# A Macaron layer on one core: the feed-forwards' output as split products in the two row halves of TensorE, their input in two runs, and another order of the work on every engine

## The chip, the core and the metric

The kernel runs on one core of a Trainium2 chip. A core has TensorE (PE: matrix products into PSUM, a memory of eight banks of 128 x 512 float32), VectorE (DVE), ScalarE (ACT), GpSimd (POOL) and SyncE (SP), which issues the transfers. The engines run side by side, each through its own instructions in order, and wait for each other only at semaphores. The metric is the device time of the one core in microseconds (us). Changes of under about 0.2% cannot be told from no change here.

## The reference

The input x is 16 x 1024 rows of 512 float32 channels. All weights are shared by the rows.

```python
def ffn(x):                                   # used twice, with the same weights
    s = x @ Win + bin_                        # 512 -> 64
    h = relu(s[..., None] * W1 + b1)          # 64 -> 64 x 16
    g = einsum('btmh,mh->btm', h, W2) + b2    # -> 64
    return g @ Wout + bout                    # 64 -> 512

def attn(x):                                  # 16 heads of 32 channels
    q, k, v = split(x @ w_attn)               # 512 -> 3 x 512
    q, k = elu(q) + 1, elu(k) + 1
    # causal linear attention:
    #   S_t = S_(t-1) + k_t v_t^T,  z_t = z_(t-1) + k_t
    #   y_t = (q_t S_t) / (q_t . z_t + 1e-6)
    return y @ w_proj

x = x + 0.5 * ffn(layernorm(x))
x = x + attn(layernorm(x))
x = x + 0.5 * ffn(layernorm(x))
```

## The kernel before

The 16384 rows are cut into 32 blocks of 512 rows, each of four tiles of 128 rows; two blocks are one batch item, so the running state starts anew in every even block. A program without loops on the device is written out for `j` = 0 to 33. In turn `j` the attention works on block `j`, the first feed-forward (called `1` or `L1`) on block `j + 2` and the second (`0` or `L3`) on block `j - 1`. Both feed-forwards of a turn share their instructions: the second lies in partitions 0 to 63, the first in 64 to 127.

Products. Everything with 512 channels (`project` for q and k, `values`, `outer` for the output projection) is done by `split3` (L916) as three products in the type float32r: high part times high part, high times low, low times high. ACT makes the high part with a copy, DVE or POOL the low part with a subtraction. All other products (`ff_in`, `ff_out`, the transposes `key` and `channels`, `den`, `spread`, `scores`, `attend`, `update`) are float32; the profile lists each of these as two matmuls, but for the transposes, of which it lists one. `ff_in` (L934) multiplies 32 x 64 pieces, so that eight of them, in four row groups and two column halves of the array, are in flight. `ff_out` (L944) is one product per tile and half: 64 rows of `ffs` (the sums g) by `wo`, 128 x 512 out.

A turn on PE: q and k of five channel groups, `ff_in`, the other three groups with `key` and `den` (the denominators q . z; `den` 0 and 1 together, 2 and 3 after six more product groups), `values`, `spread` (reciprocals of the denominators, spread to all channels), and then for each tile `scores`, `attend`, `update` and `outer`, with `channels` (transposes for the next block) in between. The eight `ff_out` stand around the last `outer`.

Between them: ACT turns q and k through `Relu` and `Exp` (L448, L450), does the normalisations (L413), the 16 `hidden` activations of the feed-forwards (L432), and the high parts and copies (L390). DVE does the 16 `hidden` sums (L647, L650), half of the masks on the scores (L702), the statistics (L616, L618), the low parts (L632), the running key sums along the rows (`zsum`, L681: a scan of 512 elements into one of the two buffers `z2`, which starts from the carried sum `zc`), the reciprocals (`rec`, L687, L689), q times the reciprocals (`qnorm`, L694) and all additions to the rows (L657, L725). POOL copies the last column of each scan to `zc` (L320), multiplies the scan by q (L322), adds the half bias (`bias`, L314), computes the deviations (L296, L298) and does the other masks (L326).

The order on each engine is written by hand. PSUM banks go to products by `give`: always the bank that was given away longest ago. The scans 2 and 3 reuse the buffers of scans 0 and 1, so they wait for `den` 0 and 1 (`s_den`, L677). `ff_out` waits for the last `hidden` sum (`s_hm`), the attention products wait for all masks of their tile (`s_am`), and the scores of a tile for the low part of the result of the tile before (`s_yl`), since these use the same four banks `att`.

Of the kernel before, what the change touches and what calls it, by code (L numbers as in the profile page):

```python
# [10 lines left out]
P = 128  # L11
TILES = 4
BLK = P * TILES
SLOTS = 5
D = 32
# [25 lines left out]
def macaron_kernel(nc, x, w_attn, w_proj, Win, bin_, W1, b1, W2, b2, Wout, bout, out):  # L41
# [9 lines left out]
    with ctx:  # L51
# [10 lines left out]
        wo = sb("wo", [P, C])  # L62
# [15 lines left out]
        ktok = [sb(f"ktok{i}", [P, C]) for i in range(2)]  # L78
# [16 lines left out]
        att = ctx.enter_context(nc.psum_tensor("att", [P, 4, 512], F32))  # L95
        psum = ctx.enter_context(nc.psum_tensor("acc_psum", [P, BLK], F32))
# [16 lines left out]
        s_fi, s_fs, s_hr, s_hm = (sem(f"s_{n}") for n in ("fi", "fs", "hr", "hm"))  # L113
# [30 lines left out]

        def reads_none(b, t):
            return b % PER == 0 and t == 0

# [7 lines left out]
        def emptied(kind, b, i):  # L155
# [15 lines left out]
            return {"v": s_v, "key": s_ktok, "xT": s_xTl, "y": s_x2, "sc": s_yl}[kind], 4 * b + i + 1  # L171
# [3 lines left out]
        def give(among, *products):  # L175

            for kind, b, i in products:
                there = on(b) and not (kind in ("o0", "o1") and (kind, b, i) in spot) and not (kind == "up" and not updates(b, i))
# [16 lines left out]
        for j in range(NB + 2):  # L195
            give(ATT + RING, ("q", j, 0), ("k", j, 0), ("k", j, 1), ("q", j, 1), ("k", j, 2))
            if on(j - 1) or on(j + 2):
                give_all("in", j, 0)
            give(ATT + RING, ("k", j, 3), ("q", j, 2), ("key", j, 0), ("den", j, 0), ("q", j, 3), ("v", j, 0),
                 ("v", j, 1), ("key", j, 1))  # L200
            for t in range(TILES):
# [3 lines left out]
            give(RING, ("v", j, 3), ("xT", j + 1, 0), ("up", j, 0), ("xT", j + 1, 1), ("key", j, 2))  # L205
            give_all("sc", j, 1)
            give(RING, ("xT", j + 1, 2), ("y", j, 0), ("xT", j + 1, 3), ("up", j, 1))
            give_all("sc", j, 2)
            give(RING, ("y", j, 1), ("up", j, 2), ("key", j, 3))
            give_all("sc", j, 3)  # L210
            give(RING, ("y", j, 2))
            give(ATT + RING, ("up", j, 3), ("o0", j - 1, 0), ("o1", j + 2, 0), ("y", j, 3), ("o0", j - 1, 1),
                 ("o0", j - 1, 2), ("o1", j + 2, 1), ("o1", j + 2, 2), ("o0", j - 1, 3), ("o1", j + 2, 3))
# [10 lines left out]
        def _(eng):  # L224
# [11 lines left out]
            for h in range(2):  # L236
                eng.dma_start(wo[M * h:M * h + M, :], Wout).then_inc(s_wo, 16)
# [30 lines left out]
        def _(eng):  # L268
# [39 lines left out]

            def bias(half, b, t):
# [6 lines left out]
            def zsum(b, g):  # L316
# [3 lines left out]
                eng.tensor_copy(zc[:, g:g + 1], z[:, BLK - 1:BLK]).then_inc(s_zc, 1)  # L320
# [11 lines left out]
            for b in range(2):  # L332
                for t in range(TILES):
                    bias(1, b, t)
# [8 lines left out]
            for j in range(NB + 2):  # L343
# [5 lines left out]
                if on(j):  # L349
                    zsum(j, 0)  # L350
# [822 lines left out]
```

## Time and profile before

| | us |
|---|---|
| median of 3 runs (lowest, highest) | 2559.25 (2556.72, 2559.64) |
| the profiled execution, its own time | 2556.46 |
| its span, first to last instruction | 2554.7 |
| PE busy | 2373.4 (93%) |
| DVE busy | 1892.7 (74%) |
| ACT busy | 1422.0 (56%) |
| POOL busy | 867.4 (34%) |

A matmul's listed duration is its latency; the next one starts before it ends. What a matmul costs its engine is the distance from its start to the next start. The mean granted clock of TensorE over the span is 0.983.

### The profile page before, as it was taken

The numbers are of one execution on the slowest core, as the hardware profiler recorded it, in microseconds if no ns is written. First come the engines' busy times: TensorE is split into PE (matmuls) and PEld (weight loads), VectorE is DVE, ScalarE is ACT, GpSimd is POOL, SyncE is SP. The second block draws the span as 40 slices with busy tenths as digits, with TensorE's granted clock in tenths as the row PEclk, the third lists the DMA queues.
The fourth block names the chain that finished last, engine by engine and source line by source line (L and its number), as shares of the span: only waits on it lengthen the run. The fifth ranks groups of instructions, "written<-read, shape, count | busy, mean of one in ns | idle before, by whom it ended". The sixth has DMA issues, their size and how long they took to land.

```text
span 2554.7 us, 75807 instructions
## 1 busy us (share of the span) xinstructions
PE 2373.4 (93%) x33282; PEld 1799.6 (70%) x33282; DVE 1892.7 (74%) x3248; ACT 1422.0 (56%) x2248; POOL 867.4 (34%) x996
## 2 busy tenths in 40 slices
PE   2799999999999999999999999999999999999995
PEld 1577777777777777777777777777777777777773
DVE  4578777778777778777777877777877777877755
ACT  3456565556565555556555656555656555556544
POOL 4332333333333333233333233333333333323221
PEclk8899999999999999999999999999999999999997
DMA  5000011001011111001110001111100111000000
GB/s 161 1 2 25 12 35 35 35 35 35 2 35 35 35 35 35 18 19 35 35 35 35 35 2 35 35 35 35 35 3 34 35 35 35 35 18 2 18 18 34
DMA packets 39355, 76.97 MB, mean 30 GB/s; under 512 B 4081, under 2 KB 4081, under 8 KB 39026
## 3 DMA queue, kind: packets, MB, share of 16 engines
q1 hardware_dynamic: 39026, 72.12, 8.2%
q8 instruction: 263, 4.31, 0.7%
q14 instruction: 66, 0.54, 0.1%
HBM read 38.56 MB, written 33.55 MB: 28 GB/s over the span
## 4 chain that ended last, share of the span: by engine, by line
PE 86%; DVE 5%; ACT 4%; issue 3%; SPq 0%; POOL 0%; DMA 0%; DVEq 0%; POOLq 0%
PE bank L916 31%; PE att L916 27%; PE att L934 6%; PE att L1010 6%; PE att L1035 4%; PE att L944 3%; DVE yl L632 3%; ACT yh L390 2%; PE att L1026 2%; PE bank L951 2%; PE att L981 1%; PE att L968 1%; PE bank L944 1%; DVE acc_psum L650 1%; ACT v L390 1%
## 5 line engine op out<-in xcount | busy, mean ns | idle before, releaser
L413 ACT ACTIVATE xhat<-res,nmr,rstd 128x512 f32<-128x512 f32 x384 | 303.0, 806 | 324.2 <-DVE nmr L623 297.0
L432 ACT ACTIVATE ffr<-ffs,b1c,w1c 128x512 f32<-128x512 f32 (+1 forms) x544 | 430.6, 810 | 17.5 <-DVE acc_psum L650 7.9
L650 DVE SCALAR_TENSOR_TENSOR acc_psum<-ffr,w2c,acc_psum 128x512 f32<-128x512 f32 (+1 forms) x476 | 354.4, 745 | 49.4 <-ACT ffr L432 34.2
L326 POOL TENSOR_SCALAR_AFFINE_SELECT A<-A 128x512 f32<-128x512 f32 x256 | 158.7, 637 | 683.7 <-ACT A L390 683.7
L314 POOL TENSOR_TENSOR res<-res,hbout 128x512 f32<-128x512 f32 x256 | 325.1, 1288 | 127.6 <-ACT xhat L413 127.6
L616 DVE BATCH_NORM_STATS2 st<-res 128x6 f32<-128x512 f32 x384 | 261.7, 682 | 17.1 <-DMA res<-in_L_attn_x_dram 8.8
L916 PE MATMUL att<-xh,wa_h 128*128 128x512 f32 x560 | 228.8, 408 | 15.4 <-DVE xl L632 15.4
L390 ACT ACTIVATE A<-att 128x512 f32<-128x512 f32 x256 | 142.5, 596 | 145.8 <-PE att L1010 143.4
L916 PE MATMUL att<-xl,wa_h 128*128 128x512 f32 x560 | 221.9, 396 | 0.0
L916 PE MATMUL att<-xh,wa_l 128*128 128x512 f32 x560 | 221.8, 396 | 0.0
L702 DVE TENSOR_TENSOR A<-att,tri 128x512 f32<-128x512 f32 x256 | 171.9, 683 | 57.2 <-PE att L1010 57.1
L934 PE MATMUL att<-xf,win 32*64 32x128 f32 x8192 | 149.8, 281 | 61.5 <-issue 41.0
L670 DVE SCALAR_TENSOR_TENSOR kT<-bank,kT 128x512 f32<-128x512 f32 x67 | 46.4, 692 | 208.8 <-ACT kT L450 208.7
L296 POOL TENSOR_SCALAR nmr<-mv 128x4 f32<-128x4 f32 x96 | 22.1, 230 | 520.2 <-DVE mv L618 520.1
L934 PEld LDWEIGHTS att<-xf,win 32*64 32x64 f32 x8192 | 135.1, 136 | 83.2 <-issue 75.4
L916 PE MATMUL bank<-xh,wa_h 128*128 128x512 f32 x464 | 186.9, 403 | 1.6 <-issue 1.6
L390 ACT ACTIVATE yh<-att 128x512 fp32r<-128x512 f32 x128 | 76.6, 598 | 193.0 <-PE att L1035 192.9
L916 PE MATMUL bank<-xl,wa_h 128*128 128x512 f32 x464 | 183.3, 395 | 0.3 <-issue 0.3
L916 PE MATMUL bank<-xh,wa_l 128*128 128x512 f32 x464 | 183.2, 395 | 0.0
L640 DVE STREAM_TRANSPOSE xf<-xhat 128x512 f32<-128x512 f32 x256 | 171.6, 689 | 9.5 <-ACT xhat L413 9.4
L448 ACT ACTIVATE kT<-bank 128x512 f32<-128x512 f32 x67 | 40.1, 598 | 246.9 <-PE bank L916 246.9
L320 POOL COPY zc<-z 128x1 f32<-128x1 f32 x128 | 79.8, 624 | 280.7 <-DVE z L681 265.5
(112 smaller groups left out, 5649.3 us busy)
## 6 DMA issues: line engine op xcount, KB each, us to landing
res<-in_L_attn_x_dram SPq DMA_DIRECT2D x32, 1024.0 KB, 5.3
out_dram<-res SPq DMA_DIRECT2D x32, 1024.0 KB, 4.3
kT<-in_L_attn_w_attn_dram SPq DMA_DIRECT2D x1, 1024.0 KB, 5.4
qT<-in_L_attn_w_attn_dram SPq DMA_DIRECT2D x1, 1024.0 KB, 7.6
v<-in_L_attn_w_attn_dram SPq DMA_DIRECT2D x1, 1024.0 KB, 10.7
A<-in_L_attn_w_proj_dram SPq DMA_DIRECT2D x4, 256.0 KB, 11.6
win<-in_L_ffn_Win_dram SPq DMA_DIRECT2D x4, 128.0 KB, 6.1
wo<-in_L_ffn_Wout_dram SPq DMA_DIRECT2D x2, 128.0 KB, 4.6
```

What stands on the lines that cost most here:

```text
L314: eng.tensor_tensor(r[:, t, :], r[:, t, :], hbout[:, :], ALU.add).then_inc(s_bias[half], 1)
L326: eng.affine_select(out=A[:, h, :, :], in_=A[:, h, :, :], compare_op=ALU.is_ge, fill=0.0, base=0, pattern=[[0, 4], [1, P]], channel_multip ...
L390: eng.activation(dst, src, ACT.Copy).then_inc(done, 1)
L413: eng.activation(xhat[t % 2][:, :], res[b % SLOTS][:, t, :], ACT.Identity, bias=nmr[:, n, t:t + 1], scale=rstd[:, n, t:t + 1]).then_inc(s_ ...
L432: eng.activation(ffr[i % 2][p, :], ffs[p, :], ACT.Relu, bias=b1c[p, i:i + 1], scale=w1c[p, i:i + 1]).then_inc(s_hr, 1)
L616: eng.bn_stats(st[:, n, t, :], r[:, t, :]).then_inc(s_bn[n], 1)
L640: eng.transpose(xf[slot][:, t, :, :].rearrange("p c i -> p (c i)"), xhat[t % 2][:, :]).then_inc(s_tr[half], 1)
L650: eng.scalar_tensor_tensor((ffs if i == INNER - 1 else psum)[p, :], r[p, :], w2c[p, i:i + 1], psum[p, :], ALU.mult, ALU.add).then_inc(s_hm, 1)
L702: eng.tensor_tensor(A[:, h, :, :], att[:, h, :].rearrange("p (g i) -> p g i", g=4), tri[:, :].unsqueeze(1).to_broadcast([P, 4, P]), ALU.mu ...
L916: op = eng.matmul(o, l, r, start=first and i == 1, stop=final and i == n)
L934: op = eng.matmul(att[M * n:M * n + M, r, 0:P], win[d, c, :], xf[n][d, :, c, :], start=c == 0, stop=c == C // D - 1)
L1010: op = eng.matmul(att[:, h, g * P:g * P + P], kT[d, g, w], qT[d, g, w], start=True, stop=True)
```

## The change

The three products of `ff_out`. The sums g no longer go to `ffs`: the last `hidden` sum stays in PSUM, ACT copies it as high part (`ffh`), DVE subtracts for the low part (`ffl`), and `ff_out` does `ffh` by `wo_h`, `ffh` by `wo_l` and `ffl` by `wo_h` for both feed-forwards, alternating between the two row halves of the array. `ffh` and `ffl` lie in the buffers `yh[0]` and `yl[0]`. The weights `wo_h` and `wo_l` are made once at the start, by ACT and POOL.

`ff_in` is issued in two runs of 64 products, with `den` 0 and 1, half of `values` 1 and `key` 0 between them. The copy to `zc` moves from POOL to DVE (`carry`), and is done only in even blocks. `key` of the last tile of a batch item is left out, since its update is not used. There is one buffer `ktok` in place of two. `values` of tile 0 comes first in a turn, `ff_out` last but for `channels` 3. ACT, DVE, POOL and the bank list are reordered to fit. In the diff, `zsum` is POOL's, the first `sums` and `key` are ACT's, the last `hidden` line, the second `sums` and `carry` are DVE's, and all below are PE's.

```diff
+        ffh, ffl = (y[0][:, :, :].rearrange("p g n -> p (g n)") for y in (yh, yl))
...
             def zsum(b, g):
                 z = z2[:, g % 2, :]
                 e.wait_ge(s_scan, 4 * b + g + 1)
                 e.wait_ge(s_elu[0], 4 * b + g + 1)
-                eng.tensor_copy(zc[:, g:g + 1], z[:, BLK - 1:BLK]).then_inc(s_zc, 1)
-                e.wait_ge(s_zc, 4 * b + g + 1)
+                if carries(b):
+                    e.wait_ge(s_zc, carried(b, g))
                 eng.tensor_tensor(z, qT[:, g, :], z, ALU.mult).then_inc(s_zq, 1)
...
+            def sums(j):
+                p = halves(j)
+                e.wait_ge(s_hm, hid(j, INNER - 1))
+                if j >= 0:
+                    e.wait_ge(s_po, 4 * min(j, NB - 1) + 3)
+                copy(ffh[p, :], psum[p, :], s_uh)
...
             def key(b, t):
-                e.wait_ge(s_kt, 4 * b + t + 1)
...
+                e.wait_ge(s_kt, nth_update(b, t))
+                e.wait_ge(s_up, nth_update(b, t) - 1)
+                copy(ktok[:, :], bank[spot["key", b, t][0]][:, :], s_ktok)
...
-                eng.scalar_tensor_tensor((ffs if i == INNER - 1 else psum)[p, :], r[p, :], w2c[p, i:i + 1], psum[p, :],
+                eng.scalar_tensor_tensor(psum[p, :], r[p, :], w2c[p, i:i + 1], psum[p, :],
                                          ALU.mult, ALU.add).then_inc(s_hm, 1)
+            def sums(j):
+                p = halves(j)
+                e.wait_ge(s_uh, j + 2)
+                lo_part(ffl[p, :], psum[p, :], ffh[p, :], s_ul)
...
+            def carry(b, g):
+                e.wait_ge(s_scan, 4 * b + g + 1)
+                eng.tensor_copy(zc[:, g:g + 1], z2[:, g % 2, BLK - 1:BLK]).then_inc(s_zc, 1)
...
-            def ff_in(j):
-                take_all("in", j, 0)
+            def ff_in(j, part):
+                if part == 0:
+                    take_all("in", j, 0)
...
-                for c in range(C // D):
+                n_c = C // D // PARTS
+                for c in range(n_c * part, n_c * part + n_c):
...
-            def ff_out(half, b, t, j):
-                o = take(f"o{half}", b, t)
-                slot = 0 if half and b == 0 else half
-                here = slice(M * slot, M * slot + M)
-                e.wait_ge(s_hm, hid(j, 15))
-                e.wait_ge(s_wo, 32)
-                eng.matmul(o, ffs[here, t * P:t * P + P], wo[here, :], start=True, stop=True).then_inc(s_fo[half], 1)
+            def ff_out(j, t, slots=(0, 1)):
+                which = ((1, 0), (1, 1)) if j < 0 else ((0, j - 1), (1, j + 2))
+                outs = [(n, *which[n]) for n in slots if on(which[n][1])]
+                o = [take(f"o{half}", b, t) for n, half, b in outs]
+                e.wait_ge(s_ul, j + 2)
+                e.wait_ge(s_wol, 1)
+                w = slice(t * P, t * P + P)
+                for i, (l, r) in enumerate(((ffh, wo_h), (ffh, wo_l), (ffl, wo_h))):
+                    for k, (n, half, b) in enumerate(outs):
+                        d = slice(M * n, M * n + M)
+                        op = eng.matmul(o[k], l[d, w], r[d, :], start=i == 0, stop=i == 2)
...
             def values(b, t, part):
+                e.wait_ge(s_xTl, 4 * b + t + 1)
...
+                if on(j - 1) or on(j + 2):
+                    ff_out(j, 0)
+                    ff_out(j, 1)
+                    ff_out(j, 2)
+                    ff_out(j, 3)
+                if on(j + 1):
+                    channels(j + 1, 3)
```

Three places show the order. The first is PE around the input of the feed-forwards (`xf`, `win`), in an even block of the kernel before; `xh`, `wa_h` and so on are q and k, `x64` or `x128` counts products.

```order
L916 MATMUL bank<-xh,wa_h 128x512
L916 MATMUL bank<-xl,wa_h 128x512
L916 MATMUL bank<-xh,wa_l 128x512
L934 MATMUL att<-xf,win 64x128 x128
L916 MATMUL bank<-xh,wa_h 128x512
L916 MATMUL bank<-xl,wa_h 128x512
```

The same place on PE in the changed kernel (`z`, `heads_of` is `den`; `ident`, `kT` is `key`; `wa_h`, `xh` with the result first is `values`):

```order
L967 MATMUL bank<-xh,wa_l 128x512
L987 MATMUL att<-xf,win 64x128 x64
L1029 MATMUL bank<-z,heads_of 32x128 x8
L967 MATMUL bank<-wa_h,xh 128x512
L967 MATMUL bank<-wa_l,xh 128x512
L967 MATMUL bank<-wa_h,xl 128x512
L967 MATMUL bank<-wa_h,xh 128x512
L967 MATMUL bank<-wa_l,xh 128x512
L967 MATMUL bank<-wa_h,xl 128x512
L1061 MATMUL bank<-ident,kT 128x128 x4
L987 MATMUL att<-xf,win 64x128 x64
L1029 MATMUL bank<-z,heads_of 32x128 x8
```

The run of 128 has become two of 64, each followed at once by a pair of `den`; between them stand six products and one transpose group, where before 30 products stood between the two pairs of `den`.

The second place is PE at the end of a turn. Before, in an odd block (`yh`, `wp_h` is `outer` 3; two `ff_out` stand ahead of its twelve products):

```order
L916 MATMUL att<-wp_h,yh 128x512
L916 MATMUL att<-wp_l,yh 128x512
L916 MATMUL att<-wp_h,yl 128x512
L944 MATMUL att<-wo,ffs 128x512 x3
L944 MATMUL bank<-wo,ffs 128x512 x3
L916 MATMUL att<-xh,wa_h 128x512
```

The end of a turn on PE in the changed kernel, in an even block (`wo_h`, `yh` is `ff_out`; `v`, `ktok` is `update` 3):

```order
L967 MATMUL att<-wp_h,yl 128x512
L1108 MATMUL att<-v,ktok 32x32 x16
L1003 MATMUL att<-wo_h,yh 128x512 x2
L1003 MATMUL att<-wo_l,yh 128x512 x2
L1003 MATMUL att<-wo_h,yl 128x512 x2
L1003 MATMUL bank<-wo_h,yh 128x512 x2
L1003 MATMUL bank<-wo_l,yh 128x512 x2
L1003 MATMUL bank<-wo_h,yl 128x512 x2
```

All `ff_out` now stand in one piece behind `outer` 3, 24 products in twelve pairs.

The third place is DVE at the scans 2 and 3 (`z<-kT`) of an even block. Before (`rden` is `rec`, `acc_psum` is `hidden`):

```order
L670 SCALAR_TENSOR_TENSOR kT<-bank,kT 128x512
L670 SCALAR_TENSOR_TENSOR qT<-bank,qT 128x512
L681 SCALAR_TENSOR_TENSOR z<-kT 128x512 x2
L647 TENSOR_SCALAR acc_psum<-ffr,w2c,b2c 128x512
L670 SCALAR_TENSOR_TENSOR qT<-att,qT 128x512
L650 SCALAR_TENSOR_TENSOR acc_psum<-ffr,w2c,acc_psum 128x512 x3
L687 TENSOR_SCALAR rden<-att 128x128
```

DVE at the same scans in the changed kernel (`zc<-z` is `carry`):

```order
L709 SCALAR_TENSOR_TENSOR qT<-att,qT 128x512
L709 SCALAR_TENSOR_TENSOR qT<-bank,qT 128x512
L721 SCALAR_TENSOR_TENSOR z<-kT 128x512
L726 COPY zc<-z 128x1
L721 SCALAR_TENSOR_TENSOR z<-kT 128x512
L726 COPY zc<-z 128x1
L731 TENSOR_SCALAR rden<-bank 128x128
L733 RECIPROCAL rden<-rden 128x128
L681 TENSOR_SCALAR acc_psum<-ffr,w2c,b2c 128x512
L738 TENSOR_TENSOR qT<-att,qT 128x4x128 x4
```

The reciprocals follow the scans directly, and the `hidden` sums, four of which stood around them, come later, among the masks of the attention.

## Rows read from the trace of the kernel before

**Rows 1.** The page's first part: busy us of each engine over the span.
```profile
PE 2373.4 (93%) x33282; PEld 1799.6 (70%) x33282; DVE 1892.7 (74%) x3248; ACT 1422.0 (56%) x2248; POOL 867.4 (34%) x996
```

**Rows 2.** Busy time in one turn and in its attention (columns: window, length, then engines).
```profile
1166.21:1242.08 75.87, 73.39 (x1048) 55.73 (x1051) 57.97 (x101) 43.10 (x69) 26.17 (x31) 1.00 0.09 30
1192.80:1219.60 26.80, 26.12 (x550) 20.80 (x551) 23.11 (x44) 17.35 (x29) 9.96 (x13) 1.00 0.01 3
```

**Rows 3.** Waits of PE over the span: us in total, times, longest.
```profile
PE att L934 <- issue: 41.0, 33, 2.5
PE att L1010 <- DVE yl L632: 19.1, 35, 0.6
PE att L981 <- ACT v L390: 14.7, 32, 0.6
```

**Rows 4.** Timeline, even block, PE at `ff_out`: start, duration, engine, operation.
```profile
1219.77 1.12 PE L944 MATMUL bank<-wo,ffs 64*128 64x512 f32 x2
1220.98 1.12 PE L944 MATMUL att<-wo,ffs 64*128 64x512 f32 x2
1222.04 0.50 PE L916 MATMUL att<-wp_h,yh 128*128 128x512 f32 x1
...
1225.04 0.69 PE L944 MATMUL att<-wo,ffs 64*128 64x512 f32 x1
1225.05 0.69 PE L944 MATMUL bank<-wo,ffs 64*128 64x512 f32 x1
1225.57 0.59 PE L944 MATMUL att<-wo,ffs 64*128 64x512 f32 x1
...
1227.82 0.50 PE L916 MATMUL att<-xh,wa_h 128*128 128x512 f32 x1
```

**Rows 5.** Timeline, odd block, PE at `ff_out`.
```profile
1296.75 1.13 PE L944 MATMUL bank<-wo,ffs 64*128 64x512 f32 x4
1298.25 0.50 PE L916 MATMUL att<-wp_h,yh 128*128 128x512 f32 x1 [0.37 <-DVE yl L632]
...
1301.24 1.55 PE L944 MATMUL att<-wo,ffs 64*128 64x512 f32 x5
...
1304.02 0.51 PE L916 MATMUL att<-xh,wa_h 128*128 128x512 f32 x1
```

**Rows 6.** Timeline, PE from `ff_in` to `key` and `den` of block 15.
```profile
1242.01 3.34 PE L934 MATMUL att<-xf,win 32*64 32x128 f32 x217
1246.81 0.91 PE L934 MATMUL att<-xf,win 32*64 32x128 f32 x39 [1.46 <-issue]
1247.65 0.50 PE L916 MATMUL bank<-xh,wa_h 128*128 128x512 f32 x1
1247.98 0.39 PE L916 MATMUL bank<-xl,wa_h 128*128 128x512 f32 x1
1248.21 0.40 PE L916 MATMUL bank<-xh,wa_l 128*128 128x512 f32 x1
...
1253.35 0.60 PE L999 MATMUL bank<-ident,kT 128*128 128x128 f32 x4
1253.88 0.64 PE L968 MATMUL att<-z,heads_of 128*32 128x128 f32 x16
```

**Rows 7.** The page's queues: the one that carries instructions (packets, MB, share).
```profile
q8 instruction: 263, 4.31, 0.7%
```

**Rows 8.** Timeline, DVE and POOL at scans 2 and 3.
```profile
1179.34 2.33 DVE L681 TENSOR_TENSOR_SCAN z<-kT 128x512 f32<-128x512 f32 x2
1180.62 1.03 POOL L320 COPY zc<-z 128x1 f32<-128x1 f32 x1 [6.20 <-DVE z L681]
1181.73 1.30 POOL L322 TENSOR_TENSOR z<-qT,z 128x512 f32<-128x512 f32 x1
```

**Rows 9.** All POOL copies of L320: ns min/median/max.
```profile
L320 POOL COPY zc<-z x128: 181/614/1093, 109.8 to 2473.6; 128x1 f32<-128x1 f32 x128
```

**Rows 10.** Timeline, DVE at the start: ten `hidden` sums in a row.
```profile
46.05 8.49 DVE L650 SCALAR_TENSOR_TENSOR acc_psum<-ffr,w2c,acc_psum 128x512 f32<-128x512 f32 x10
```

More of the change, by code:

```diff
@@ L14 @@
 SLOTS = 5
+PARTS = 2
 D = 32
@@ L177, in give @@
             for kind, b, i in products:
-                there = on(b) and not (kind in ("o0", "o1") and (kind, b, i) in spot) and not (kind == "up" and not updates(b, i))
+                there = on(b) and not (kind in ("o0", "o1") and (kind, b, i) in spot) and not (kind in ("up", "key") and not updates(b, i))
                 if there:
@@ L493, in _ @@
                 hidden(-1, i)
+            sums(-1)
             e.wait_ge(s_wa[0], 16)
@@ L506, in _ @@
                 if on(j):
+                    values(j, 0)
+                    project(j, 1, 0)
                     project(j, 0, 0)
@@ L520, in _ @@
                     project(j, 0, 1)
+                    project(j, 1, 3)
+                    project(j, 0, 2)
+                    project(j, 0, 3)
+                if on(j - 1) or on(j + 2):
+                    ff_bias(j)
+                if on(j):
+                    key(j, 0)
+                if on(j - 1) or on(j + 2):
+                    hidden(j, 0)
+                if on(j):
+                    values(j, 1)
+                if on(j - 1) or on(j + 2):
+                    hidden(j, 1)
+                    hidden(j, 2)
                 if on(j + 1):
@@ L738, in _ @@
                 hidden(-1, i)
+            sums(-1)
             for b in range(2):
@@ L788, in _ @@
                     qnorm(j, 3)
+                if on(j + 3):
+                    stats(L1, j + 3, 1)
+                if on(j - 1) or on(j + 2):
+                    hidden(j, 1)
+                    hidden(j, 2)
+                if on(j):
+                    mask(j, 0, 1)
+                    mask(j, 0, 3)
+                if on(j - 1) or on(j + 2):
+                    hidden(j, 3)
+                if on(j + 3):
+                    stats(L1, j + 3, 2)
+                if on(j):
+                    update(j, 0)
+                if on(j - 1) or on(j + 2):
+                    hidden(j, 4)
+                if on(j):
+                    ysplit(j, 0)
+                if on(j - 1) or on(j + 2):
+                    hidden(j, 5)
+                if on(j):
+                    mask(j, 1, 3)
+                    mask(j, 1, 1)
                 if on(j - 1) or on(j + 2):
@@ L1062, in _ @@
             eng.matmul(o[:, :], tri[0:1, :], z2[0:1, 1, :], start=True, stop=True).then_inc(s_mbout, 1)
-            ff_in(-1)
+            for part in range(PARTS):
+                ff_in(-1, part)
             for b in range(2):
                 for t in range(TILES):
-                    ff_out(1, b, t, -1)
+                    ff_out(-1, t, (b,))
             for t in range(TILES):
@@ L1097, in _ @@
                     values(j, 3, 0)
+                    update(j, 0)
+                    attend(j, 0)
                     values(j, 3, 1)
```

421 lines of the change are left out of this document (197 added, 224 removed).

## The prediction

> **What bounds the kernel now.** I read the page's busy shares first, then the windows of one turn and of its attention, then PE's waits, then PE's timeline around the pieces that the diff touches. TensorE is the engine to look at: 93% busy over the span [rows 1], and 73.39 of the 75.87 us of a steady turn [rows 2]. It waits little, and what it waits for is named [rows 3]: 41.0 us inside `ff_in` for its own instructions ("issue"), 19.1 us before `scores` for the low part `yl`, 14.7 us before `spread` for ACT's copy of `v`. So an edit is worth what it takes from PE's own sequence, as long as the others keep up. VectorE is the next: 57.97 us of a turn, but 23.11 of 26.80 in the attention [rows 2]. There its order, not its average, can become the bound. All prices below are distances between starts on PE, per turn, for 32 turns.
>
> **The output products.** Before, an even turn spends 1219.77 to 1222.04 and 1225.04 to 1227.82 on `ff_out` [rows 4]: 2.27 + 2.78 = 5.05 us. An odd one spends 1296.75 to 1298.25 and 1301.24 to 1304.02 [rows 5]: 1.50 + 2.78 = 4.28. The mean is 4.67. In the second piece two matmuls start 10 ns apart, one in each row half, and the next pair follows 0.53 us later [rows 4]; six pairs took 2.78, 0.46 each. So the halves do run beside each other, in float32. A float32r product with 512 columns takes 1248.21 - 1247.98 = 0.23 us of PE [rows 6], and all rows that show it use the full array; a pair of them in two row halves is not in this trace. Between 0.23 for a pair (as parallel as float32) and 0.46 (one after the other) I take 0.23, because the float32 pairs are the nearest row. 24 products in 12 pairs: 2.8 us. Gain 1.87.
>
> **The input in two runs.** The pause in `ff_in` is 41.0 / 33 = 1.24 us each time [rows 3]; in block 15 PE had done 217 matmuls in 3.34 us, then stood for 1.46 [rows 6]. A matmul has a weight load, so 434 instructions went in 3.34 us, 130 per us. The instruction queue moved 263 packets [rows 7] for 2 x 33282 instructions [rows 1], 253 each. I read the pause as PE outrunning these packets: 253 instructions take 1.95 us at that pace, and with 1.46 of pause the next packet came 3.4 us after the one before. A run of 64 products is 256 instructions in 2.09 us (half of 1247.65 - 1242.01 - 1.46), with `den` behind it 288, and then 20 instructions fill some 2.1 us. Two packet borders come closer than 3.4 us only if the first lies in the first 35 instructions of a run or some 11 to either side: 57 of 253 places, with about 0.9 us each, twice a turn. That leaves 0.40. Gain 0.84; bounds 0 and 1.24.
>
> The Trainium skill speaks against this reading (Runtime: NRT & Kernel Launch, Instruction fetch mechanics): it gives PE a store of 2048 instructions, refilled in blocks of 256, and calls a border "mostly hidden". The trace agrees with the block size (253) and not with the hiding: PE stands 1.46 us after 434 instructions. By the page the pause would have another cause and splitting need not remove it; that is the second rival.
>
> **One excursion less.** Going from full-array products to small ones and back costs time: the first product after `ff_in` takes 1247.98 - 1247.65 = 0.33 instead of 0.23 [rows 6]. With as much on the way out, 0.2 for each excursion. Counted in PE's order there were 13 in a turn and are 12: the split adds one, but each `den` pair now stands behind a run of `ff_in`, and `ff_out` is one piece. Gain 0.2. The Trainium skill says that a change of tiling mode drains TensorE (TensorEngine Tiling (Array Packing), Key Properties), which speaks against a split; by the rule alone the split would cost 0.2 more, and 0.2 is what it costs before the neighbours are counted.
>
> **Left out and moved away.** One `key` group in two turns: 1253.88 - 1253.35 = 0.53, half of it 0.27 [rows 6]. The wait for `yl` before the last `scores`, 19.1 / 32 = 0.60, goes, because half of `outer` 1 and one or two `key` groups now stand between `attend` 2 and `scores` 3. The wait at `spread`, 14.7 / 32 = 0.46, goes, because `values` 1 no longer sits in the four banks that `spread` needs; what is late next there are the reciprocals, about 1.3 us behind `den` 3, covered by the half of `values` 1 (1.6).
>
> Gains: 1.87 + 0.84 + 0.20 + 0.27 + 1.06 = 4.24 us.
>
> **What it costs: the key sums.** `den` 0 releases scan 2. From there: two scans 2.33, then POOL's two products of 1.30, one after the other [rows 8], with three handovers some 5.3 us until `den` 3 can go. POOL can't start between the scans: its copy of one column began 1180.62 - 1179.34 = 1.28 us after scan 2 did and ended with scan 3, after 1.03 us [rows 8], while the quickest such copy took 181 ns [rows 9]. PE has only `den` 1 (0.29), half of `values` 1 (6 x 0.23 + 0.2 = 1.6), `key` (0.53), the second run (2.09) and `den` 2 (0.29) between: 4.8. Before it had 7.7. So PE newly waits about 0.5; queued behind `den` 3 are everything up to `spread`, the reciprocals and `qnorm`. `carry` on DVE may itself be held up by one POOL product (1.30) in even turns. I take 0.6; bounds 0 (POOL's first product slips ahead of scan 3) and 1.3. The Trainium skill has this as a lock on a shared port that the loser waits out, for DVE instructions with two SBUF inputs (SBUF — State Buffer, Who interferes with whom); the 1.03 us agree. Without such a lock the wait would be 0 and the sum 19 us lower.
>
> **Masks and the tail.** Between `scores` 0 and `attend` 0 stand now half of `values` 3 and `update` 0, 2.0 us, where before stood all of `values` 3 and a transpose, 3.5. The last mask follows two `hidden` sums on DVE. At 23.11 / 44 = 0.53 us an instruction [rows 2], being one instruction late is 0.5; I take 0.2, bounds 0 and 0.6. At the end of a turn `ff_out` waits for a new chain: last `hidden`, ACT's high part, DVE's low part. From `attend` 3 to `ff_out` PE has a transpose 0.5, 18 products 4.2, `update` 0.4 and an excursion 0.2: 5.3 us. DVE has two or three `hidden` sums, two low parts, one addition with its two statistics and the new subtraction, 9 instructions of 0.53, 4.8, partly waiting for ACT. I take 0.25, bounds 0 and 1.5. Costs: 0.6 + 0.2 + 0.25 = 1.05.
>
> **The rest** lies beside other work. ACT gets one copy a turn with 43.10 of 75.87 busy. POOL loses 128 copies (26.17 busy). DVE gets the subtraction, and the four small copies in half of the turns: under 59 of 73 us. `ff_out` in a row instead of spread makes the additions on DVE lag PE by some 5 us, but `values` 0, which needs one tile only, gives 2.8 us before q needs all. At the start two copies and the subtraction add about 2 us to a chain that PE waits on, and `values` 0 before q and k takes 1.4 off. At the end the same chain adds 1.3 and shorter products give it back. Together +1.
>
> **The sum.** 4.24 - 1.05 = 3.19 us a turn, 102 us in 32. The profiled execution took 2556.46: 2556.46 - 102 + 1 = 2455.5. The median of the runs shown is 2.8 us higher, so I say 2457 (-4.0%).
>
> **Rivals.** First: the float32r halves run one after the other. 24 x 0.23 = 5.6 instead of 2.8, +90 us: 2547. Against it stand the float32 pairs [rows 4]. 6%.
>
> Second: the pause stays, because it is not the packets, or because the second run meets it again. +0.84 x 32 = 27: 2484. For it: one pause in each run, 33 of 33 [rows 3]. Against it: it lies 434 instructions into the run, not at its start. 12%.
>
> Third, slower than before: VectorE becomes the bound of the attention. The changed order puts twelve `hidden` sums between `scores` 0 and the end of `attend` 3, where nine stood, takes out two low parts and one addition with two statistics, and PE wants the stretch in 25 us instead of 26.8. That is 42 instructions instead of 44, at 0.53 us [rows 2] 22.1, a slack of 2.9. But ten `hidden` sums in a row took 8.49, 0.85 each [rows 10]; if all 16 of a turn cost that and not 0.53, DVE has 5.1 more to do, 2.2 more than its slack, and 1.2 for two waits on PE's scores (0.6 each) can't be caught up: 3.4 late, and with that the tail costs its upper 1.5 and not 0.25. It decides from 3.19 on: (3.4 + 1.25 - 3.19) x 32 = 47 us slower, 2603. Against it: only eight of the sums follow one another directly. 7%, of which 5 slower than before.
>
> Fourth: all covers hold, no new wait and no pause: 1.45 x 32 = 46 less, 2411; near it, about 2425, 15%. My forecast with its own spread (2440 to 2480) has 57%, other mixtures 3%.
>
> **Range and chances.** 2420 to 2510 leaves out the first and third rivals (13%) and a bit of the fourth. Of what can be told from no change (0.2%, 5 us): faster 0.93, same 0.02, slower 0.05.
>
> **What would show it.** PE's waits: no or few "issue" in `ff_in`, both rows of `scores` on `yl` and `spread` on `v` gone, a new wait of `den` on POOL's product of 0.5 us. In the timeline, `ff_out` pairs with starts 10 ns apart and 0.23 to the next pair, 2.8 us from first to last. The distance between turns is 72.7 instead of 75.87. I am wrong on DVE if PE waits for `A`, `yl` or `ffl` (rows of `scores`, `attend`, `outer`, `ff_out`) by over 1 us a turn, and on the pairs if `ff_out` takes over 5 us.

## The result, and the profile after

The changed kernel takes 2463.41 us (median of four, 2461.27 to 2464.55). The kernel before took 2559.02 beside it. The ratio is 0.9627 (95% interval 0.9610 to 0.9644), 3.7% faster. The prediction said 2457. The profiled execution took 2462.28, with a span of 2460.6.

The page's busy shares, which answer to [rows 1], and its chain of the work that ended last, by engine:

```profile
PE 2326.5 (95%) x33474; PEld 1796.0 (73%) x33474; DVE 1908.5 (78%) x3346; ACT 1433.4 (58%) x2267; POOL 813.7 (33%) x869
...
PE 51%; DVE 23%; issue 15%; POOL 7%; ACT 3%; SPq 1%; DVEq 0%; DMA 0%; POOLq 0%
```

TensorE's busy share hardly moved (93 to 95%), because both its work and the time shrank. The chain moved a lot: before it was 86% PE and 5% DVE. Now it changes engines all the time, a sign that the others have less slack behind PE (how much, dve1 and dve3 show below). The stretches that answer to [rows 2] (from one `ff_in` to the next, and from `scores` 0 to the end of `attend` 3; columns as there):

```profile
1143.31:1215.88 72.57, 71.69 (x1049) 55.49 (x1048) 58.27 (x104) 43.62 (x70) 24.44 (x27) 1.00 0.09 31
1156.85:1181.79 24.94, 24.48 (x511) 18.67 (x511) 22.12 (x41) 20.06 (x33) 7.21 (x10) 1.00 0.01 3
```

A turn lost 3.3 us here, and the attention, with DVE busy 22.12 of 24.94, is tighter than before. PE's waits, answering to [rows 3], less those of the first and last block:

```profile
PE bank L1029 <- POOL z L344: 9.5, 26, 0.5
...
PE att L1097 <- DVE A L746: 5.9, 15, 0.7
PE att L987 <- issue: 3.2, 2, 2.0
PE bank L1029 <- issue: 3.0, 5, 1.2
PE att L1088 <- DVE A L746: 2.3, 14, 0.2
```

All three rows of [rows 3] are gone: 41.0 us of issue waits in `ff_in` are 3.2 (2.0 of it once, at the start), and those for `yl` before `scores` and for `v` before `spread` are 1.1 and none. New are `den` behind POOL (9.5) and `attend` behind the masks (8.2). The output products of block 14, answering to [rows 4]:

```profile
1186.99 0.50 PE L1003 MATMUL att<-wo_h,yh 64*128 64x512 f32 x2
1187.33 0.41 PE L1003 MATMUL att<-wo_l,yh 64*128 64x512 f32 x2
1187.57 0.40 PE L1003 MATMUL att<-wo_h,yl 64*128 64x512 f32 x2
1187.81 0.39 PE L1003 MATMUL bank<-wo_h,yh 64*128 64x512 f32 x2
...
1188.97 0.39 PE L1003 MATMUL bank<-wo_h,yl 64*128 64x512 f32 x1
1188.97 0.39 PE L1003 MATMUL att<-wo_h,yl 64*128 64x512 f32 x1
1189.33 0.50 PE L1003 MATMUL att<-wo_h,yh 64*128 64x512 f32 x2
...
1190.22 0.66 PE L1012 MATMUL att<-ident,xhat 128*128 128x128 f32 x4
```

Two products share a row ("x2"), and the next two follow 0.23 to 0.24 us later. The first pair takes 0.34, the pair before tile 3 stands 0.36 and its successor 0.33 (the bank comes late from VectorE), and the way out takes another 0.1: 3.23 in all.

To see where the time went I added up the distances between starts on PE for 20 turns of each kernel (blocks 4 to 24), by function. A wait counts to the group ahead of it.

| us a turn | before | after |
|---|---|---|
| `ff_in` (before with 1.23 of issue wait) | 5.37 | 4.05 |
| `ff_out` | 4.67 | 3.21 |
| `key` (before with the waits for `yl` and `v`, 1.02) | 3.52 | 1.80 |
| `channels` | 2.02 | 1.77 |
| `den` (after with 0.39 of waits) | 1.15 | 1.82 |
| `attend`, `update` (after with 0.28 of waits) | 6.72 | 7.51 |
| split products, `scores`, `spread` | 52.32 | 52.38 |
| sum (before 75.77) | 75.77 | 72.55 |

Over the whole kernel, from block 0's `spread` to block 31's, a turn is 75.85 before and 72.74 after: 31 x 3.11 = 96.4 us less. The first `spread` starts at 132.66 instead of 127.35, 5.3 us later, and what follows the last one is 73.0 instead of 76.0. -96.4 + 5.3 - 3.0 = -94.1, the difference of the spans.

### The profile page after: what moved, and what is told of

It is laid out like the page before. It is cut to its first block, busy times and chain, and to the rows that moved or that the text cites. A ratio compares the mean times of both kernels' runs of the same rounds, so it can differ in the third digit from the quotient of the medians.

```text
span 2460.6 us, 76187 instructions
## 1 busy us (share of the span) xinstructions
PE 2326.5 (95%) x33474; PEld 1796.0 (73%) x33474; DVE 1908.5 (78%) x3346; ACT 1433.4 (58%) x2267; POOL 813.7 (33%) x869
## 4 chain that ended last, share of the span: by engine, by line
PE 51%; DVE 23%; issue 15%; POOL 7%; ACT 3%; SPq 1%; DVEq 0%; DMA 0%; POOLq 0%
PE bank L967 20%; PE att L967 11%; DVE acc_psum L684 6%; PE att L1072 5%; POOL z L344 5%; DVE st L650 4%; PE att L1097 4%; DVE qT L738 3%; PE att L987 3%; DVE res L696 2%; DVE A L746 2%; PE att L1003 2%; DVE yl L666 2%; PE att L1042 1%; PE bank L1012 1%
## 5 line engine op out<-in xcount | busy, mean ns | idle before, releaser
L684 DVE SCALAR_TENSOR_TENSOR acc_psum<-ffr,w2c,acc_psum 128x512 f32<-128x512 f32 (+1 forms) x510 | 382.3, 750 | 34.5 <-ACT ffr L449 15.4
L344 POOL TENSOR_TENSOR z<-qT,z 128x512 f32<-128x512 f32 x128 | 189.4, 1500 | 165.0 <-DVE zc L726 84.0
L967 PE MATMUL att<-xh,wa_h 128*128 128x512 f32 x524 | 207.2, 395 | 0.0
L967 PE MATMUL att<-xh,wa_l 128*128 128x512 f32 x524 | 207.2, 395 | 0.0
L967 PE MATMUL att<-xl,wa_h 128*128 128x512 f32 x524 | 207.2, 395 | 0.0
L967 PE MATMUL bank<-xh,wa_l 128*128 128x512 f32 x500 | 197.7, 395 | 0.0
L967 PE MATMUL bank<-wa_h,xh 128*128 128x512 f32 x440 | 192.4, 437 | 0.0
L967 PE MATMUL bank<-wa_l,xh 128*128 128x512 f32 x440 | 174.3, 396 | 0.0
L967 PE MATMUL bank<-wa_h,xl 128*128 128x512 f32 x440 | 173.9, 395 | 0.0
L967 PE MATMUL bank<-wp_h,yh 128*128 128x512 f32 x388 | 172.5, 445 | 0.0
```

The costliest lines, as they stand in the source:

```text
L344: eng.tensor_tensor(z, qT[:, g, :], z, ALU.mult).then_inc(s_zq, 1)
L684: eng.scalar_tensor_tensor(psum[p, :], r[p, :], w2c[p, i:i + 1], psum[p, :], ALU.mult, ALU.add).then_inc(s_hm, 1)
L967: op = eng.matmul(o, l, r, start=first and i == 1, stop=final and i == n)
```

## The experiments

"Before" was timed again beside each group of kernels, and its median lay between 2554.0 and 2559.0, so a difference of under 5 us between kernels of different groups says nothing by itself. The trace is finer: the table has the first `spread` (what the start costs) and the mean turn over blocks 0 to 31, both from each kernel's profile.

| kernel | median us | ratio to before (95%) | first `spread` | turn |
|---|---|---|---|---|
| changed kernel | 2463.4 | 0.9627 (0.9610-0.9644) | 132.66 | 72.74 |
| serial | 2464.1 | 0.9639 (0.9625-0.9653) | 133.33 | 72.78 |
| samerows | 2538.6 | 0.9927 (0.9911-0.9944) | 133.07 | 75.16 |
| ffout32 | 2479.5 | 0.9699 (0.9683-0.9715) | 133.96 | 73.14 |
| onerun | 2484.9 | 0.9722 (0.9707-0.9736) | 130.54 | 73.60 |
| poolcarry | 2466.8 | 0.9649 (0.9634-0.9663) | 133.28 | 72.90 |
| scanpsum | 2450.0 | 0.9592 (0.9579-0.9605) | 132.23 | 72.32 |
| start1 | 2458.4 | 0.9625 (0.9612-0.9638) | 127.69 | 72.77 |
| start2 | 2452.0 | 0.9600 (0.9587-0.9613) | 121.42 | 72.76 |
| dve1 | 2471.4 | 0.9675 (0.9662-0.9688) | 132.02 | 73.00 |
| dve3 | 2493.3 | 0.9751 (0.9736-0.9765) | 132.30 | 73.72 |
| upd | 2469.8 | 0.9660 (0.9646-0.9675) | 131.84 | 72.96 |
| best | 2445.0 | 0.9562 (0.9547-0.9576) | 121.70 | 72.47 |

### Do the halves run side by side? (serial, samerows)

```
-                for i, (l, r) in enumerate(((ffh, wo_h), (ffh, wo_l), (ffl, wo_h))):
-                    for k, (n, half, b) in enumerate(outs):
+                for k, (n, half, b) in enumerate(outs):
+                    for i, (l, r) in enumerate(((ffh, wo_h), (ffh, wo_l), (ffl, wo_h))):
```

> The changed kernel, but of each tile's six output products the three of one half stand first and then the three of the other, instead of alternating. Theory (the gain rests on two products, one in each row half, running side by side): the 12 pairs of a turn at 0.23 us become 24 products that each take 0.23 us alone, so 12 x 0.23 = 2.8 us more in a turn, of which the engines that PE waits for may give back a part: 60 to 90 us slower, 2525 to 2550 us, and ff_out about 6.0 us instead of 3.2. Rival (two products of different row halves overlap in whatever order they stand, or the gain did not come from there): within 10 us of 2463.

Nothing changed: the turn is 72.78, `ff_out` 3.20 against 3.19. The rival held, and the trace of serial says how. Its PE timeline at tile 2:

```profile
1190.17 0.39 PE L1003 MATMUL bank<-wo_h,yh 64*128 64x512 f32 x1
1190.18 0.39 PE L1003 MATMUL att<-wo_h,yh 64*128 64x512 f32 x1
1190.40 0.39 PE L1003 MATMUL bank<-wo_l,yh 64*128 64x512 f32 x1
1190.41 0.39 PE L1003 MATMUL att<-wo_l,yh 64*128 64x512 f32 x1
```

In the program two other products of the same half (`wo_l` by `yh`, `wo_h` by `yl`) lie between the two of the first pair, and yet these start 10 ns apart. Either PE starts a product of the free half ahead of those queued for the other, or the starts say nothing. To tell these apart the next kernel takes away the two row halves (and so leaves out the true products of one of them):

```
-                        d = slice(M * n, M * n + M)
+                        d = slice(0, M) if j >= 0 else slice(M * n, M * n + M)
```

> The changed kernel, but from block 0 on both halves' output products read rows 0 to 63 of the hidden sum and of Wout, so that no two of them lie in different row halves (block j+2 gets the sums of block j-1: this kernel leaves its true products out). Banks, waits and order are those of the changed kernel. The run that put the halves in blocks of three changed nothing and its trace still showed starts 10 ns apart; this one takes away the row halves themselves. Theory (two products run side by side because they lie in different row halves, however they stand): 24 x 0.23 = 5.5 us instead of 3.2 in a turn, 31 x 2.3 = 70 us slower, less what engines off PE's path catch up: 2510 to 2535 us. Rival (the starts 10 ns apart are an artefact of how ends are modelled and a 64-row product is simply shorter): within 8 us of 2463.

The turn is 2.43 us longer, the time 75 us. Its `ff_out` takes 5.80 (median of the turns) instead of 3.19; the PE timeline at tile 2:

```profile
1224.20 0.39 PE L1003 MATMUL bank<-wo_h,yh 64*128 64x512 f32 x1
1224.43 0.39 PE L1003 MATMUL att<-wo_h,yh 64*128 64x512 f32 x1
1224.67 0.39 PE L1003 MATMUL bank<-wo_l,yh 64*128 64x512 f32 x1
1224.90 0.39 PE L1003 MATMUL att<-wo_l,yh 64*128 64x512 f32 x1
```

Each product now takes its own 0.23. So the overlap is real, is worth 75 us, and needs different row halves, but no alternation within a tile. The Trainium skill (TensorEngine Tiling (Array Packing), Key Properties) has tiles that "operate independently"; these runs agree, and show it with two products standing between.

### What did splitting the products bring? (ffout32)

```
-                for i, (l, r) in enumerate(((ffh, wo_h), (ffh, wo_l), (ffl, wo_h))):
...
-                        op = eng.matmul(o[k], l[d, w], r[d, :], start=i == 0, stop=i == 2)
...
+                    op = eng.matmul(o[k], ffs[d, w], wo_h[d, :], start=True, stop=True)
```

> The changed kernel, but each tile and half has one float32 product again (left operand ffs, right one Wout as loaded) instead of three split ones; ACT's copy of the hidden sum goes to ffs, and the two subtractions of low parts are left in (they give zeros that nothing reads). Theory A (a float32 product is two passes of 0.43 us on its row half, and those of two halves run side by side when they stand in turn): 4 x 0.86 = 3.4 us against 3.2 now: within 12 us of 2463, so the gain in ff_out came from the pairing, and splitting the products bought almost nothing. Theory B (float32 products do not overlap, or only in part, as before's 4.67 us for them shows): 1.2 to 3.6 us more in a turn, 40 to 115 us slower.

Between the two theories, nearer A: `ff_out` takes 3.64 (each turn within 0.04) instead of 3.19, the turn 0.40 more, the time 16 us. So float32 products overlap too, at 0.43 a pass for a pair. Of the 1.46 us that `ff_out` gave up, 4.67 to 3.64 (1.03) came with the new place and order and 3.64 to 3.21 (0.43) with the split. For that a copy on ACT and a subtraction on DVE had to be added.

### One run or two (onerun)

```
-                if on(j - 1) or on(j + 2):
-                    ff_in(j, 0)
                 if on(j):
                     den(j, 0)
...
                 if on(j - 1) or on(j + 2):
+                    ff_in(j, 0)
                     ff_in(j, 1)
```

> The changed kernel, but all 128 products of ff_in stand at the second place, after key 0 and before den 2, as one run. Theory (the pause of PE in the middle of before's ff_in came from the row of small instructions being long, and the split took it away): the issue wait of about 1.2 us is back in each turn; the 0.3 us wait before den 3 goes, since the scans get more time: net 0.6 to 1.2 us a turn, 20 to 40 us slower, 2483 to 2503 us, and the page shows a wait 'issue' at L987 x about 30. Rival (the pause went because of something else, such as where the run stands): within 8 us of 2463, no issue wait.

As the theory had it: 21.5 us slower. The wait is back, 31 times, and the POOL wait before `den` is gone. PE's waits and its timeline at one run:

```profile
PE att L987 <- issue: 39.6, 31, 2.6
```

```profile
1154.76 3.12 PE L987 MATMUL att<-xf,win 32*64 32x128 f32 x200
1158.97 1.13 PE L987 MATMUL att<-xf,win 32*64 32x128 f32 x56 [1.09 <-issue]
```

PE stops after 200 matmuls here and after 217 in [rows 6], at 130 instructions per us. The run's length matters, not where it stands. That fits packets of instructions that come too slowly. No kernel tried the packets by themselves, but the kept traces have the time of each packet of the instruction queue. All 35 pauses of over 0.3 us in `ff_in` and `den` of onerun end 1.20 to 1.59 us after such a packet has landed, and so do 29 of the 31 in the kernel before (1.26 to 1.53), while the packets start 6.6 and 7.1 us apart (median). So PE goes on when a packet has come, and the packets are the cause as far as coinciding times can show it. The shortest distance between two packet starts in the kernel before is 3.35 us, against the 3.4 that the prediction worked out. Why a packet is not asked for sooner stays open.

### The key sums (poolcarry, scanpsum)

The first hunk is POOL's, the second VectorE's, of whose four copies (0 to 3) the first stands here.

```
                 if carries(b):
+                    eng.tensor_copy(zc[:, g:g + 1], z2[:, g % 2, BLK - 1:BLK]).then_inc(s_zc, 1)
                     e.wait_ge(s_zc, carried(b, g))
...
-                if on(j) and carries(j):
-                    carry(j, 0)
```

> The changed kernel, but the one-column copy that keeps the key sum for the next block stands on POOL again, between its wait for the scan and its multiplication (as before), and VectorE's four copies in an even turn are gone. Theory (a POOL copy beside a VectorE scan takes 1.03 us, and den now stands close behind the scans): in even turns den 2 and 3 come 0.9 to 1.9 us later, in odd turns nothing: 16 x 0.9 to 16 x 1.9, 15 to 30 us slower, 2478 to 2493 us. Rival (other work on PE hides it): within 5 us of 2463.

The theory was too high, and the rival's 5 us hold. It is 3.4 us by the medians, and 0.17 us a turn by the trace; the `den` wait grew from 9.5 to 13.8. All POOL copies of this kernel (ns min/median/max):

```profile
L343 POOL COPY zc<-z x64: 177/184/1182, 116.3 to 2314.2; 128x1 f32<-128x1 f32 x64
```

At least half of them take the short time here, where [rows 9] had a median of 614 ns; the long ones reach what [rows 8] showed beside a scan. Moving the copy to VectorE brought 0.17 x 31, some 5 us.

```
-                eng.tensor_tensor_scan(z2[:, g % 2, :], kT[:, g, :], kT[:, g, :], ...
+                eng.tensor_tensor_scan(z2[:, g % 2, :], kT[:, g, :], psum[:, :], ...
```

> The changed kernel, but the second operand of the four scans, which the bypass leaves unused, is read from PSUM (acc_psum) instead of from kT, so that a scan reads one stream from SBUF and one from PSUM. Theory (two SBUF streams of VectorE shut POOL out for as long as the scan runs, and this is what makes den wait 0.3 us a turn): POOL's multiplication for group 2 starts during the scan of group 3, the POOL wait before den goes, 5 to 10 us faster, 2453 to 2458 us. Rival (den's wait is the chain of scan and multiplication itself, or PE is held by VectorE in any case): within 3 us of 2463; and if a scan with a PSUM operand is longer, up to 5 us slower.

13.5 us faster, more than expected, 0.42 us in each turn. The scans take the same (means of 1.22 and 1.26, in the changed kernel 1.24 and 1.27), but POOL is free beside them. POOL's group of multiplications in the changed kernel, then in this one (busy us, mean ns), and then the same place in the timeline of each, in the same order:

```profile
L344 POOL TENSOR_TENSOR z<-qT,z 128x512 f32<-128x512 f32 x128 | 189.4, 1500 | 165.0 <-DVE zc L726 84.0 <-DVE z L721 68.5 <-DVE qT L709 12.5
```

```profile
L344 POOL TENSOR_TENSOR z<-qT,z 128x512 f32<-128x512 f32 x128 | 162.6, 1286 | 167.1 <-DVE zc L726 82.5 <-DVE z L721 70.0 <-DVE qT L709 13.3
```

```profile
1147.23 1.23 DVE L721 TENSOR_TENSOR_SCAN z<-kT 128x512 f32<-128x512 f32 x1
1147.48 3.27 POOL L344 TENSOR_TENSOR z<-qT,z 128x512 f32<-128x512 f32 x2 [4.08 <-DVE zc L726]
...
1149.96 0.43 PE L1029 MATMUL bank<-z,heads_of 128*32 128x128 f32 x8
1150.81 0.43 PE L1029 MATMUL bank<-z,heads_of 128*32 128x128 f32 x8 [0.42 <-POOL z L344]
```

```profile
1141.84 1.22 DVE L721 TENSOR_TENSOR_SCAN z<-kT,acc_psum 128x512 f32<-128x512 f32 x1
1142.09 2.61 POOL L344 TENSOR_TENSOR z<-qT,z 128x512 f32<-128x512 f32 x2 [4.08 <-DVE zc L726]
...
1144.58 0.64 PE L1029 MATMUL bank<-z,heads_of 128*32 128x128 f32 x16
```

Two multiplications take 2.61 instead of 3.27, the mean is 1286 instead of 1500 ns, and `den` 2 and 3 run as one piece without a wait. Over blocks 4 to 24 `den` takes 1.34 us a turn here and 1.82 in the changed kernel. So the whole gain stands at this place: a wait is listed from the modelled end of the product before it, and the 0.42 above is 0.85 from start to start, where a `den` alone takes 0.29. The second operand is ignored by the operation, but it was read all the same. The Trainium skill (SBUF — State Buffer, Who interferes with whom) has this as a lock on a port, held by a VectorE operation with two inputs from SBUF; this pair of kernels differs in nothing else and agrees.

### The start (start1, start2)

At the changed kernel's start, VectorE and POOL:

```profile
42.76 1.26 POOL L329 TENSOR_TENSOR wo_l<-z,wo_h 128x512 fp32r<-128x512 f32 x1 [5.82 <-ACT wo_h L411]
...
44.31 1.04 POOL L316 TENSOR_TENSOR rstd<-nmr,mhalf 128x4 f32<-128x4 f32 x1
...
45.32 4.49 POOL L325 TENSOR_TENSOR wa_l<-kT,wa_h 128x2048 fp32r<-128x2048 f32 x1
45.38 4.45 DVE L657 SCALAR_TENSOR_TENSOR nmr<-mv,rstd 128x4 f32<-128x4 f32 x1 [8.43 <-POOL rstd L316]
49.75 0.80 DVE L681 TENSOR_SCALAR acc_psum<-ffr,w2c,b2c 128x512 f32<-128x512 f32 x1
```

An operation on 4 columns, whose like takes 0.26 us in the mean of all 96 in this kernel, takes 4.45 us because POOL began a long one 0.06 us earlier.

```
+            rstds(L1, 2)
             wout_lo()
-            rstds(L1, 2)
             weights_lo(1)
```

> The changed kernel, but POOL's subtraction for wo_l stands behind the rstds of block 2 instead of ahead of them. Theory (the 5.3 us later start comes from there: POOL waits for ACT's copy of Wout, so the rstds end while its 4.49 us subtraction of w_attn's low part begins, and VectorE's 4-column nmr is held up by that for 4.45 us): the nmr of block 2 takes 0.2 to 1.3 us, the first hidden product starts some 4 us sooner and everything after it: 3.0 to 4.7 us faster, 2459 to 2460.5 us; block 0's spread at about 128.3 us instead of 132.66. Rival (the start is then held by the next thing, such as the low parts of the weights on POOL, which end at the same time as now): within 1 us of 2463.4.

In the trace this is as the theory had it, and a little more: the first hidden product of VectorE starts at 45.26 instead of 49.75, the first `spread` at 127.69 (-5.0), and the turns are unchanged within 0.03. The medians give -5.1 us, but the ratios overlap: by the times alone it isn't settled.

start2 adds, on VectorE, that the `nmr` of block 1 comes behind the four subtractions instead of ahead of them:

```
-                shift(L2, b)
+                if b == 0:
+                    shift(L2, b)
             for t in range(TILES):
                 channels(0, t)
+            shift(L2, 1)
```

> start1, and VectorE's four subtractions for xl of block 0 stand ahead of the nmr of block 1 (L2), which POOL's subtraction for wp_l holds up for 4.45 us. Theory (PE's first products wait for xl and nothing else): another 3 to 5 us, 2454 to 2457 us in all. Rival (POOL's subtraction for the value weights ends no sooner, about 88.3 us, and every product of block 0 waits for it or is waited for by ACT): at most 1 us beyond start1.

6.4 us below start1, timed against the same runs of before; the first `spread` is at 121.42, 11.2 sooner than in the changed kernel. PE's first product of the attention now starts at 82.54 instead of 93.44 (start1: 88.97), and its wait, for `xl` in the changed kernel, is now one for POOL:

```profile
82.54 0.77 PE L969 MATMUL att<-wa_h,xh 128*128 128x512 f32 x1 [7.25 <-POOL wa_l L325]
```

The rival's subtraction is indeed next in line, but it ended sooner than the rival had it.

### How much slack VectorE has (dve1, dve3)

```
+            def extra(n):
...
+                eng.bn_stats(scr[:, :], hbout[:, :]).then_inc(s_scr, 1)
```

> The changed kernel with one more operation on VectorE in each turn (bn_stats of a constant 128x512 tile into a tile that nothing reads, 0.68 us each by the trace) in the attention, ahead of channels(j+1, 1). It asks how near VectorE is to setting the time: the chain that ends last now passes through VectorE for 23% of the span (before 5%). Theory A (VectorE has spare time in the attention, its waits there take the extra up): within 4 us of 2463. Theory B (from here on VectorE is the bound for a part of the turn): 32 x 0.68 = 22 us slower, or a part of it that says how much of the turn is bound.

> The changed kernel with three more operations of 0.68 us on VectorE in each turn, spread over the attention (ahead of ysplit 0, channels 0 and channels 1 of the next block). One cost 8 us where 22 was the most, 0.25 us a turn. Theory A (the slack is used up from the first one on, so the second and third cost in full): 8 + 2 x 22 = 52 us slower, 2515 us. Theory B (each one is a third hidden wherever it stands, since ACT, POOL and PE are waited for in between): 25 us, 2488 us. By the prediction's third rival VectorE had 2.9 us of slack in the attention: then 3 x 0.68 = 2.04 would cost nothing.

One extra operation costs 0.26 us a turn (38% of its 0.68), three cost 0.98 (48% of 2.04). Neither "free" nor "in full" holds. What grows most is one wait of PE (1.1 us in all in the changed kernel), in dve1 and then dve3:

```profile
PE att L1080 <- DVE yl L667: 7.8, 17, 0.9
```

```profile
PE att L1083 <- DVE yl L667: 27.2, 46, 1.1
```

`scores` waits for `yl`, the row that the change had cleared. The third rival's working gave VectorE 2.9 us of slack in the attention, and by busy time there are 2.82 (24.94 - 22.12). But that is not slack for work at these places: the first 0.68 us already shows in the time.

### VectorE's order at `ff_out`, and the parts together (upd, best)

The statistics of `outer` 3 stood ahead of both.

```
+                if on(j) and updates(j, 3):
+                    update(j, 3)
                 if on(j - 1):
                     ff_out(0, j - 1, 0)
-                if on(j) and updates(j, 3):
-                    update(j, 3)
+                if on(j):
+                    stats_of_sum(L3, j, 3)
```

> The changed kernel, but VectorE's update of S for tile 3 stands ahead of its first addition of the output products, and outer 3's statistics behind it. Theory (the last pair of ff_out waits 0.13 us for its bank in each turn, and PE is the bound there): ff_out takes 3.07 instead of 3.19, at most 0.12 x 32 = 4 us faster, 2459 to 2463 us. Rival (VectorE is behind PE in this stretch, and the order of its own work changes nothing): within 1.5 us of 2463.

Both theories failed: 0.22 us a turn slower. `ff_out` itself went from 3.19 to 3.16, so the bank did come sooner. But the statistics now stand between VectorE's first and second addition, and the bank of the second is the one that `channels` 3 needs. PE at that place in block 14, in upd and in the changed kernel: from the last pair of products to `channels` 0.49 against 0.33, and from there to the first projection 0.59 against 0.41.

> All that helped together: start2 (wo_l behind the rstds, xl of block 0 ahead of the nmr), scans with their second operand in PSUM, and VectorE's order of upd. If the parts add up: 2463.4 - 11.4 - 13.5 and 0 to 4 more, 2434.5 to 2438.5 us. If a part of them paid for the same wait (both start2 and the scans change only what PE waits for at different places, so none is known): up to 2443 us.

2445.0, ratio 0.9562 (0.9547 to 0.9576), whose interval lies below that of the changed kernel: 18 us faster, and the lowest median here, though its interval overlaps scanpsum's. It missed what was expected, 2434.5 to 2438.5 and 2443 at most. The start (121.70) and the scans' gain are both in it; its turn is 72.47, 0.16 over scanpsum's, and the trace puts this at upd's place: `channels` takes 1.95 us a turn as in upd, where scanpsum has 1.77. Without upd some 31 x 0.16 = 5 us less is an estimate, not run.

## Why the prediction was right, step by step

The turn came out as worked: 72.7 predicted, 72.74 measured. In the 20 turns of the table the gain is 3.22 where the sum was 3.19. But part of that is luck, since the terms are off both ways.

- **Output products, 1.87 predicted, 1.46 measured.** The mechanism was right (samerows) and its price of 0.23 a pair too, with starts 10 ns apart or in one row. I had counted 12 pairs and nothing at the ends: 0.1 on the way in, 0.1 on the way out, and 0.2 around the pair whose bank comes late make 3.2 of 2.8 (in upd, where that bank is in time, all pairs between the first and the last stand at 0.23 to 0.24). And 0.43 of it only is owed to float32r (ffout32).
- **The pause, 0.84 predicted, 1.14 measured** (1.23 gone, 0.09 back). onerun brings it back at its old size, and the packets' times fit the reading. The remainder of 0.40 was too careful: the pause appears in 5 of 32 turns, behind the second run, at `den`. The Trainium skill (Runtime: NRT & Kernel Launch, Instruction fetch mechanics) calls the cost of a border between blocks of instructions "mostly hidden". The 1.28 us of onerun, 31 times and each ending behind the landing of a packet, do not agree with that.
- **The waits for `yl` and `v`, 1.06 predicted, 1.02 measured.** Both went from the turns.
- **Key group and excursion, 0.47 predicted.** What is left for them and all small things is 3.22 - 1.46 - 1.14 - 1.02 + 0.57 = 0.17 (0.35 with `den` priced from start to start, see below). `den` took 0.28 and `attend` with `update` 0.51 more a turn beside their waits, while `channels` gave 0.25 and `key` 0.43 more than its missing group: neighbours and borders that I had not priced one by one.
- **Costs, 1.05 predicted, 0.57 measured.** `den` behind POOL 0.30 by the list of waits, instead of 0.6. It is VectorE's second operand from SBUF that holds POOL, as predicted (scanpsum). Without that `den` takes 0.48 less from start to start, the turn 0.42 less: by this count the costs are 0.75. "19 us" was said for this case; 13.5 were measured. Masks 0.27 instead of 0.2. The tail 0 instead of 0.25: PE waits for the low part of the hidden sum only at the start and at the end.
- **Start and end, +1 predicted, +5.4 measured** (94.1 against 32 x 3.11 = 99.5). This step failed: "two copies and the subtraction add about 2 us" priced the work that was added, and not what it is moved against. ACT's copy of Wout holds POOL, so POOL goes from its `rstd` straight into a subtraction of 4.49 us, and VectorE's tiny operation, which needs that `rstd` and starts 60 ns later, is shut out until the subtraction is done (start1: 5.0 of the 5.3). Of the 6.8 us between the sum, 2455.5, and the profiled 2462.28 it is 4.4; most of the rest is the turn, 3.11 us shorter over the whole kernel and not 3.19.

Of the rivals, the first (halves one after the other, +90) would have come out at +75 if it had been the case. The second did not come true; onerun makes its case, with 2484.9 against the 2484 that the rival named. That closeness is luck: the rival adds 27 us to 2457, onerun 21.5 to 2463.4, and onerun also loses the `den` wait. The third did not come true either: VectorE did not become the bound of the attention. But the slack that its working gave VectorE was not there (dve1). The fourth (2411 to 2425) asked for a gain of 4.64 us a turn. The costs that it left out measured 0.57 (0.75 with `den` from start to start), and even with the `den` wait gone, scanpsum's turn is 3.53 below before's: the missing part lies in the gains.

## What to carry to other kernels

Products that use half of the array's rows should stand next to products of the other half. Within the six products of a tile the order was free, and here the place and order brought more (1.03 us a turn) than splitting the products did (0.43). Look at what an unused operand reads: a scan's ignored second input cost 13 us here until it came from PSUM. Where a small VectorE operation started 60 ns behind a long one of POOL it took 4.45 us, so put the long ones behind what others wait for. And an engine's idle time in a stretch is not its slack: of 0.68 us more work on VectorE 0.26 came out in the time, beside 2.82 us of idle time.

## What the runs showed of the hardware

- PE started a 64-row product of one half 10 ns after one of the other with two other products between them in the program; with both in the same rows each took its own 0.23 us.
- A float32 product of 64 rows and 512 columns is two passes of 0.43 us, shared with its partner in the other half; a float32r one is a single pass of 0.23.
- A VectorE scan of 1.22 us with both inputs in SBUF held up POOL; with one input in PSUM it took as long, and POOL's multiplication beside it took its own time (mean 1286 ns, against 1500). POOL's 4.49 us subtraction held up a 128 x 4 operation of VectorE for 4.45 us.
- In a stretch of small matmuls PE took 130 instructions per us and then stood 1.1 to 1.5 us after 400 to 434 of them; runs of 256 mostly passed without. In onerun each of the 35 pauses ended 1.20 to 1.59 us after the landing of a 16 KB packet of the instruction queue.
